# One core, graph attention with 32 batches: the permuted bias is made by GpSimd from the natural one, in place of a second load

## What is computed

```python
q = (x @ Wq.T).reshape(B, N, 12, 32); k = (x @ Wk.T)...; v = (x @ Wv.T + bv)...
a = einsum('bnhd,bmhd->bhnm', q, k) * SCALE + adj[:, None, :, :]
pad_mask = all(a == 0, axis=-1)
a = nan_to_num(softmax(where(pad_mask, -inf, a), axis=-1))
o = einsum('bhnm,bmhd->bnhd', a, v).reshape(B, N, 384)
out = layernorm(x + o @ Wo.T + bo)
```

## Time and profile before

| | |
|---|---|
| three runs, median (lowest, highest) | 763.73 us (762.37, 765.3) |
| profiled execution, device time | 762.95 us |
| its span | 761.0 us |
| mean granted clock of TensorE | 0.978 |
| TensorE busy | 716.0 us, 94% |
| ScalarE busy | 615.5 us, 81% |
| VectorE busy | 587.8 us, 77% |
| GpSimd busy | 453.1 us, 60% |
| moved by DMA | 193.00 MB, mean 254 GB/s |

### The profile page before, as it was taken

One profiled execution on the slowest core, in us unless ns is written; L12 is line 12 of the kernel. 1 busy time (PEld: TensorE's weight loads), 2 busy tenths in 40 slices (PEclk: granted clock), 3 DMA queues, 4 the chain that ended last, 5 costly groups with the idle time before them and its releaser, 6 DMA issues.

```text
span 761.0 us, 22949 instructions
## 1 busy us (share of the span) xinstructions
PE 716.0 (94%) x7480; PEld 609.5 (80%) x7480; DVE 587.8 (77%) x2216; ACT 615.5 (81%) x1991; POOL 453.1 (60%) x518
## 2 busy tenths in 40 slices
PE   6889999999999999999999999999999999998753
PEld 5777888888888888888888888888888888886532
DVE  2677788888888888888888888888888888788821
ACT  2678888888988898888888988888889889888721
POOL 3345676766666676666666766666667666665331
PEclk7999999999999999999999999999999999999985
DMA  8087788888877877878778788777887887777631
GB/s 260 3 284 243 265 286 278 271 283 274 275 262 258 284 243 282 299 273 285 263 258 283 239 286 286 253 261 275 300 285 238 287 281 246 283 275 257 234 102 43
DMA packets 92664, 193.00 MB, mean 254 GB/s; under 512 B 4736, under 2 KB 51584, under 8 KB 84352
## 3 DMA queue, kind: packets, MB, share of 16 engines
q1 hardware_dynamic: 92544, 191.52, 74.7%
HBM read 111.80 MB, written 79.69 MB: 252 GB/s over the span
## 4 chain that ended last, share of the span: by engine, by line
PE 87%; DMA 3%; DVE 3%; POOL 2%; issue 2%; ACT 2%; SPq 0%; ACTq 0%; POOLq 0%; DVEq 0%
PE bank_b L534 45%; PE bank_a L621 12%; PE s_bank L580 11%; PE bank_t L591 9%; PE bank_c L534 9%; PE bank_c L602 2%; DVE neg L784 1%; DMA w_f<-in_wqT 1%; DMA xr<-in_x 1%; DMA sq_probT<-sq_dram 1%; POOL o_lo L346 1%; POOL kq_lo L336 1%; DMA sq_dram<-w_f 1%; ACT prob L439 1%; DVE w_f L798 0%
## 5 line engine op out<-in xcount | busy, mean ns | idle before, releaser
L439 ACT ACTIVATE prob<-neg,negmax 128x256 f32<-128x256 f32 x768 | 380.7, 501 | 40.8 <-DVE negmax L784 38.3
L784 DVE CUSTOM_DVE_ANT_0 neg<-s_bank,bias_sq 128x256 f32<-128x256 f32 x512 | 190.9, 410 | 48.9 <-PE s_bank L580 44.0
L798 DVE STREAM_TRANSPOSE w_f<-prob 128x512 f32<-128x512 f32 x256 | 173.1, 695 | 0.0
L439 ACT ACTIVATION_READ_ACCUMULATOR prob<-neg,negmax 128x1 f32 x768 | 147.9, 193 | 0.0
L336 POOL TENSOR_TENSOR kq_lo<-kq,kq_hi 128x512 fp32r<-128x512 f32 x96 | 124.2, 1293 | 7.7
L534 PE MATMUL bank_b<-xt_hi,w_hi 128*128 128x256 f32 x384 | 116.8, 304 | 7.1 <-DVE w_lo L760 3.3
L534 PE MATMUL bank_b<-xt_lo,w_hi 128*128 128x256 f32 x384 | 109.8, 286 | 0.0
L534 PE MATMUL bank_b<-xt_hi,w_lo 128*128 128x256 f32 x384 | 109.5, 285 | 0.0
L362 POOL TENSOR_SCALAR var_eps<-meanvar 128x2 f32<-128x2 f32 x32 | 7.3, 228 | 168.1 <-DVE meanvar L882 168.1
L784 DVE CUSTOM_DVE_ANT_0 neg<-s_bank,bias 128x256 f32<-128x256 f32 x256 | 92.3, 416 | 10.5 <-PE s_bank L580 10.5
L372 POOL TENSOR_TENSOR xr<-xr,bo_all 128x768 f32<-128x768 f32 x32 | 59.2, 1849 | 53.2 <-DMA xr<-in_x 53.1
(11 more groups left out here) (66 smaller groups left out, 1793.9 us busy)
## 6 DMA issues: line engine op xcount, KB each, us to landing
sq_dram<-w_f SPq DMA_DIRECT2D x64, 1024.0 KB, 6.4
sq_probT<-sq_dram SPq DMA_DIRECT2D x64, 1024.0 KB, 6.2
xt<-in_xT SPq DMA_DIRECT2D x32, 384.0 KB, 5.7
xr<-in_x SPq DMA_DIRECT2D x32, 384.0 KB, 6.1
out_y<-y_out SPq DMA_DIRECT2D x32, 384.0 KB, 6.4
bias_sq<-in_adjP SPq DMA_DIRECT2D x32, 256.0 KB, 6.4
bias<-in_adj SPq DMA_DIRECT2D x32, 256.0 KB, 6.9
w_f<-in_wkT SPq DMA_DIRECT2D x3, 192.0 KB, 4.3
```

The source lines that it names most:

```text
L439: nc.scalar.activation(prob[:, u % PROB_RING, k], neg[:, h, w.c], ACT.Exp, scale=-1.0, bias=negmax[t.p][:, w.c, h:h + 1], accum_out=sums[t ...
L784: nc.vector.tensor_tensor_reduce(out=neg[:, h, w.c], in0=s_bank[h % JH][:, w.c, :], in1=by[t.p][:, w.c, :], scale=-1.0, scalar=BIG, op0=AL ...
L798: nc.vector.transpose(sq_stage[w.g][:, :, a:a + PAIR, :, w.c].rearrange("p b h m s -> p (h m) b s"), prob[:, u % PROB_RING].rearrange("p k ...
```

## The change

`adjP` and its load are gone, the natural bias is loaded for the batch after next at the place in SP's step where the permuted load stood, and GpSimd writes `bias_sq` from `bias` with one copy a batch. The copy reads four blocks of 32 elements with a step of four elements each (`m r b -> m b r`), and writes them one behind the other. VectorE's first add of a batch waits for that copy in place of the load.

```diff
-            def load_bias_sq(t):
-                after(sp, neg_ready, t.count(H * NT, -H * NT))
-                sp.dma_start(bias_sq[t.p][:], adjP[t.c].rearrange("(c p) m -> p c m", p=P)
-                             ).then_inc(bias_sq_loaded[t.p], DMA)
-
...
-            load_bias_sq(Batch(0))
+            load_bias(Batch(0))
             load_xt(Batch(1))
             load_w(W_V, wvT)
             load_b(bv_all, bv)
-            load_bias(Batch(0))
...
-                nxt = t.later(1)
                 prev2 = t.later(-2)
-                if nxt.alive and not nxt.first:
-                    load_bias(nxt)
...
                 if nxt2.alive and not nxt2.first:
-                    load_bias_sq(nxt2)
+                    load_bias(nxt2)
...
+            def permute_bias(t):
+
+                pool.wait_ge(bias_loaded[t.p], t.loads())
+
+                after(pool, neg_ready, t.count(H * NT, -H * NT))
+                apart(pool)
+                nc.gpsimd.tensor_copy(bias_sq[t.p][:].rearrange("p c (m b r) -> p (c m) b r", m=NT, b=BLOCKS),
+                                      bias[t.p][:].rearrange("p c (m r b) -> p (c m) b r", m=NT, b=BLOCKS)
+                                      ).then_inc(bias_sq_ready, 1)
+
...
                     split_kq(nxt, "K01")
+                    permute_bias(nxt)
                 if prev2.alive:
                     deviation(prev2)
...
                 if u == 0:
-                    dve.wait_ge(bias_sq_loaded[t.p], t.loads())
+                    dve.wait_ge(bias_sq_ready, t.count(1, 1))
```

More of the change, by code:

```diff
@@ L82, in steps, with build @@
         body(Batch(c))
-def build(nc, x, xT, adj, adjP, wqT, wkT, wvT, bv, woT, bo, out):
+def build(nc, x, xT, adj, wqT, wkT, wvT, bv, woT, bo, out):
     def sb(name, shape, dt=F32):
@@ L164, in build @@
     bias_loaded = [sem(f"bias_loaded{p}") for p in range(2)]
-    bias_sq_loaded = [sem(f"bias_sq_loaded{p}") for p in range(2)]
+    bias_sq_ready = sem("bias_sq_ready")
     xt_hi_ready = sem("xt_hi_ready")
@@ L938, in _ @@
             steps(step)
-_INS = ["x", "xT", "adj", "adjP", "wqT", "wkT", "wvT", "bv", "woT", "bo"]
+_INS = ["x", "xT", "adj", "wqT", "wkT", "wvT", "bv", "woT", "bo"]
 def kernel(x, adj, L0_gnn_Wq, L0_gnn_Wk, L0_gnn_Wv, L0_gnn_bv, L0_gnn_Wo, L0_gnn_bo):
@@ L947 @@
     from concourse.bass_utils import run_bass_kernel_spmd
-    adjP = np.asarray(adj).reshape(B, N, NT, SQ, BLOCKS).transpose(0, 1, 2, 4, 3).reshape(B, N, N)
     arrays = {
-        "x": np.asarray(x), "xT": np.asarray(x).transpose(0, 2, 1), "adj": np.asarray(adj), "adjP": adjP,
+        "x": np.asarray(x), "xT": np.asarray(x).transpose(0, 2, 1), "adj": np.asarray(adj),
         "wqT": np.asarray(L0_gnn_Wq).T, "wkT": np.asarray(L0_gnn_Wk).T, "wvT": np.asarray(L0_gnn_Wv).T,
```

## The result

The changed kernel takes 770.03 us (median of 4 runs, 769.21 to 770.64), the kernel before 763.24 us (median of 4, with one run more than the table shows). The ratio is 1.0084, with a 95% interval of 1.0061 to 1.0108. So the change costs 6.8 us, 0.84%, where 7.8 us were forecast. The profiled execution has a span of 767.7 us against 761.0.

What follows compares the result with a forecast made beforehand. TensorE, with no idle time in steady batches, was taken as the bound. 26 x 0.28 = 7.3 us of delay plus 0.5 at the start made 7.8 us, so 770.75 profiled and 771.5 us as median, range 762.5 to 778.

Steps and rivals of the forecast that it cites:

- The bound: Steady batches: TensorE busy for all 21.85 us of a period, so each stall put into its queue is paid every batch.
- The mechanism: VectorE's `find_zero` cannot proceed while GpSimd's copy reads SBUF, so TensorE's `flag` waits: 0.28 us a batch.
- The copy's length: GpSimd's new copy, length d: taken as 1.06 us, from 0.61 without the step up to 1.29.
- the ratio in the Trainium skill's "GPSIMD Engine Reference": Rival on GpSimd's copy: a read step above 8 bytes costs half as much again, d = 0.83, 765.5 us; chance 0.20.
- The delay per batch: TensorE's transposes behind `flag` start later in each steady batch, by 0.28 us for a copy of 1.06 us.
- d - 0.78: Delay of TensorE's transposes in us per batch, d being the copy's length: 0.28 us at d = 1.06.
- The number of batches: Steady batches that pay the delay: 27 less batch 12, so 26 x 0.28 = 7.3 us.
- The start: Batch 0: the copy meets the delayed `w_lo`, first adds about 1.06 us later; 0.5 us reaches TensorE, bounds 0 and 1.1.
- the sum: Total added time: 7.3 us from the steady batches and 0.5 at the start, 7.8 us.
- The end: Removed transfers in the chain at start and end: gain bounded by 1.5 us, taken as 0.
- The removed load: 32 transfers of 256 KB fewer: worth 0 in the steady part, at the two ends at most 1.5 us, taken as 0.

## Why the prediction was right

**The bound.** Right. TensorE has no idle time in the steady part, and the 0.31 us put into each of its batches came out at the end.

**The mechanism.** Right, and shown: another form of `find_zero` beside the same copy, a shorter copy, a later place, or a cut in two each returned the whole loss; an overlap with another instruction kept it. That the holder has to read SBUF, as the prediction has it, is not shown, for every holder here reads it.

**The copy's length.** I took 1.06 us between 1.04 and 1.11; its median is 1.133. The nearest row, ScalarE's permuted save, was a better guide than the ratio in the Trainium skill's "GPSIMD Engine Reference", which would have led to 765.5.

**The delay per batch.** d - 0.78 gives 0.35 us for d = 1.13. Between `spread` and the transposes it is 0.33 in the mean, and the period grows by 0.31. Of this difference 0.015 us come back in the first 3 us behind `flag`, where the same instructions of TensorE follow each other a little more closely than before. `find_zero` was to take 0.78 us at d = 1.06, which is 0.85 at d = 1.13, and takes 0.84 in the mean of batches 3 to 29. The formula was a little too high and d too low, and the two errors partly cancel, which is luck: forecast 0.28, measured 0.31.

**The number of batches.** I took 26, leaving out batch 12, where GpSimd had run late. In the profile after, no split is late there, and `find_zero` is at 0.82 to 0.85 us in all 27 batches from 3 to 29. The lateness was not one execution's chance either: in both other profiles of kernels without a copy the subtraction of batch 12, too, starts 0.94 us before `find_zero` in place of 1.56. In some kernels with a copy a split is late in other batches. Why, no run tells. `find_zero` of batch 3 and that of batch 31 are 618.45 us apart (727.15 - 108.70) and were 610.20 (718.72 - 108.52): 8.25 us more, 27 x 0.306, where the sum had 7.3.

**The start.** The copy of batch 0 does meet the delayed `w_lo`, and `w_lo` goes first:

```profile
23.51 2.25 POOL L366 COPY bias_sq<-bias 128x512 f32<-128x512 f32 x1
22.42 2.35 DVE L767 SCALAR_TENSOR_TENSOR w_lo<-w_f,w_hi 128x1152 fp32r<-128x1152 f32 x1 [11.19 <-ACT w_hi L408]
25.94 0.42 DVE L786 CUSTOM_DVE_ANT_0 neg<-s_bank,bias_sq 128x256 f32<-128x256 f32 x1 [1.16 <-POOL bias_sq L366]
```

The copy stands for 2.25 us, half of it held, and the adds come 1.1 us later against the scores, as priced. What of it reaches batch 3 can't be read off, since the Wq load landed 1.4 us earlier in this execution; `find_zero` of batch 3 came 0.18 us later than before, where I had 0.5.

**The end.** From the last `find_zero` to the end of the span it is 40.6 us (767.7 - 727.15) and was 42.3. The last xr load, which stands in the chain there, landed after 5.2 us and before after 6.9. Over the other kernels' profiles this stretch has 40.4 to 43.6 us, so I take it for chance, which is not shown. 0.18 + 8.25 - 1.7 gives the 6.7 us between the spans.

**The removed load.** Taken as 0. The run without copy and second load puts it at 2.1 us, 0.9 to 3.4 by its interval. This is the term that I had sized worst, and it hid a slightly larger loss. Against the kernel with no copy, the ratios give 1.0084 / 0.9972, so that the copy by itself costs about 8.6 us, where I had 7.8. That the sum came out within 1 us of the measured 6.8 is in part luck: a cost too low by 0.8 and a gain of 2.1 left out.

## What to carry to other kernels

An engine's idle time is not enough cover for a new instruction: look at what its neighbours run beside it, and at every one of them that has little slack to the bounding engine. A tiny instruction whose printed length varied from batch to batch (0.18, 0.39, 0.61 us in the kernel before) was held, and the row that ended 0.03 us ahead of its end named the holder. Cutting the long instruction in two (0.9984) or changing the form of the short one (0.9963) was here worth as much as moving the long one (0.9995).

## What the hardware showed that I had not expected

A `tensor_scalar` of VectorE on 24 elements that falls due during a GpSimd copy or subtraction is held until that has ended (0.85 us in place of 0.18), and the same with an accumulator output is not (0.18 us). GpSimd's copy of 512 float32 elements a partition takes 0.614 us plain, 0.648 with a read step of 8 bytes, 1.133 with a read step of 16 bytes, and 1.133 with a write step of 128 bytes. And the profile books the time for which an instruction is held as that instruction's work, and the wait of the engine behind it, through its weight load, as "issue".
